# Three reorderings on VectorE in a bidirectional-WKV plus FFN kernel: four partial-weight sums, a backward scan and a low-half operand change places with their neighbours

## The reference

```python
ek  = exp(min(f, 30));  ekv = ek * f                 # k = v = f
n_t = n_{t-1} * decay + ekv_t                        # scans over time, forwards and backwards;
d_t = d_{t-1} * decay + ek_t                         # decay is one number per batch row and channel
num = nf + nb - ekv + exp(min(u + f, 30)) * f
den = df + db - ek  + exp(min(u + f, 30))
mix = sigmoid(x) * num / max(den, 1e-8) * (0.8 + 0.2 * tf)
h   = einsum('bsd,fd->bsf', mix, W1)
a   = gelu(clip(round(h / 0.1), -32768, 32767) * 0.1)
out = x + einsum('bsf,df->bsd', a, W2)
```

## Time and profile before

| | us |
|---|---|
| median of 2 runs | 1725.78 (1725.59 to 1725.98) |
| the profiled execution, its own time | 1725.98 |
| its span, first to last instruction | 1724.2 |
| PE busy in the span | 1628.7 |
| DVE busy | 1344.5 |
| ACT busy | 1027.1 |
| mean granted TensorE clock | 0.988 |

### The profile page before, as it was taken

How to read it: one execution, slowest core, us unless ns; L and a number is a source line. 1 busy time by engine, 2 the same in 40 slices (tenths; PEclk the granted TensorE clock), 3 DMA queues, 4 the chain that set the end, 5 groups by cost and what they waited for, 6 DMA issues and landing times. The chain is left out here.

```text
span 1724.2 us, 34213 instructions
## 1 busy us (share of the span) xinstructions
PE 1628.7 (94%) x13682; PEld 1341.6 (78%) x13682; DVE 1344.5 (78%) x1839; ACT 1027.1 (60%) x1635; POOL 162.2 (9%) x159
## 2 busy tenths in 40 slices
PE   1699999989899999999899999999989999999998
PEld 0234446878788888888788888888878888888887
DVE  8988796679878788698986789788987778946252
ACT  3578332655857666576756647576584757656361
POOL 0000110001020110101010020200102010110201
PEclk9799999999999999999999999999999999999999
DMA  8979985779576785959668695877958678586866
GB/s 238 250 177 297 305 307 194 252 252 286 167 183 233 226 259 152 262 179 285 207 178 242 199 263 178 196 255 216 276 164 227 205 226 243 159 263 225 217 193 132
DMA packets 163654, 386.63 MB, mean 224 GB/s; under 512 B 15200, under 2 KB 73312, under 8 KB 162528
## 3 DMA queue, kind: packets, MB, share of 16 engines
q1 hardware_dynamic: 116720, 291.29, 50.4%
q0 software_dynamic: 33200, 53.23, 18.3%
q10 hardware_dynamic: 13568, 39.85, 6.9%
HBM read 353.90 MB, written 85.98 MB: 255 GB/s over the span
## 5 line engine op out<-in xcount | busy, mean ns | idle before, releaser
L843 PE MATMUL ps<-mo,w_ring 128*128 128x256 f16 x6272 | 696.1, 273 | 10.3 <-DVE ps L1879 5.5
L843 PEld LDWEIGHTS ps<-mo,w_ring 128*128 128x128 f16 x6272 | 612.4, 98 | 85.7 <-issue 14.8
L906 PE MATMUL ps<-act,w_ring 128*128 128x256 f16 x5488 | 623.0, 275 | 22.8 <-DVE act L1958 17.7
L906 PEld LDWEIGHTS ps<-act,w_ring 128*128 128x128 f16 x5488 | 539.9, 99 | 94.2 <-DVE act L1958 19.8
L758 POOL DMA_DIRECT2D out_dram<-xy x111 | 134.6, 1360 | 1339.0 <-ACT xy L1324 773.5
L1879 DVE SCALAR_TENSOR_TENSOR ps<-sp,ps 128x512 f32<-128x512 f32 x84 | 58.1, 692 | 113.6 <-PE ps L843 61.6
L1266 ACT ACTIVATE a<-q 128x1024 f32<-128x1024 int16 x124 | 130.9, 1056 | 6.7 <-DVE act L1919 2.1
L1958 DVE SCALAR_TENSOR_TENSOR act<-tt,act 128x1024 f16<-128x1024 f32 x91 | 110.9, 1218 | 12.4 <-ACT act L1307 12.4
L784 PE MATMUL ps<-mo,w_ring 128*128 128x512 f16 x256 | 66.1, 422 | 55.6 <-DVE mo L1808 55.2
L1013 PE MATMUL ps<-act,w_ring 128*128 128x512 f16 x512 | 110.7, 379 | 0.0
L1932 DVE TENSOR_TENSOR tt<-a 128x1024 f32<-128x1024 f32 x49 | 59.9, 1223 | 61.6 <-ACT a L1266 61.6
(11 more groups left out here) (139 smaller groups left out, 1902.2 us busy)
## 6 DMA issues: line engine op xcount, KB each, us to landing
w_ring<-w1s SPq DMA_DIRECT2D x168, 512.0 KB, 5.7
w_ring<-w_half SPq DMA_DIRECT2D x74, 512.0 KB, 6.0
w_ring<-w2s SPq DMA_DIRECT2D x56, 512.0 KB, 5.1
out_dram<-xy POOLq DMA_DIRECT2D x111, 256.0 KB, 6.3
w_ring<-w2f SPq DMA_DIRECT2D x56, 384.0 KB, 4.3
V<-in_fside_dram SPq DMA_DIRECT2D x64, 256.0 KB, 4.9
R<-in_x_dram SPq DMA_DIRECT2D x64, 256.0 KB, 5.2
w_half<-in_w_dram POOLq DMA_DIRECT2D x16, 1024.0 KB, 9.9
```

The source lines that it names most:

```text
L843: mm = pe.matmul(dst[:, f, :], wp_ring[:, k, r, f, q, :], mo[:, op, q, p, :], start=(fresh and f == 0 and q == 0 and p == 0), stop=(q == K ...
L906: mm = pe.matmul(dst[:, i, :], wy_ring[:, k, i, 2 * (s - base) + j, :], ab[:, operand_at(s, op), j, p, :], start=(fresh and i == 0 and s = ...
```

## The change

In VectorE's `chained_block` three pairs of neighbours change places. Nothing is added or removed, and the lists of the other engines stay as they are.

- Edit 1, block 1 only: in the rounds s = 2, 3 and 4 `f_sums(s - 2)` comes ahead of `seed_u4(hid(n, s))`, no longer behind it. (`f_sums(3)` stays.)
- Edit 2, all blocks (it has an effect in 1 to 6): `mix(5, 2)` comes ahead of `seed_u4(hid(n, 6))`.
- Edit 3, all blocks (it has an effect in 1 to 6): `quads_lo_11(n, 6)` comes ahead of `mix(6, 1)`.

```diff
                     mix(1, s - 2)
+                    if n == 1:
+                        f_sums(s - 2)
                     if not nxt:
                         check(at + 2 * s - 4)
                         check(at + 2 * s - 3)
                     seed_u4(hid(n, s))
-                    if n == 1:
-                        f_sums(s - 2)
...
                 check(at + 3 if nxt else at + 8)
+                mix(5, 2)
                 seed_u4(hid(n, SPLIT + 2))
-                mix(5, 2)
                 mix(5, 3)
...
                 mix(6, 0)
                 seed_u4(hid(n, LAST))
+                quads_lo_11(n, SPLIT + 2)
                 mix(6, 1)
-                quads_lo_11(n, SPLIT + 2)
                 quad_sums(n, SPLIT + 2)
```

## The result

| | before | after |
|---|---|---|
| median of the runs, us | 1725.78 (2 runs) | 1739.66 (2 runs, 1738.90 to 1740.41) |
| the profiled execution, its own time | 1725.98 | 1740.08 |
| its span | 1724.2 | 1738.2 |
| mean granted TensorE clock | 0.988 | 0.981 |

The ratio is 1.0085, with an interval of 1.0060 to 1.0109: 13.9 us more, where 17.2 us were forecast. The time of 1739.7 us lies inside the range, 3.3 us under the predicted number. Of its terms, edit 3's was right in kind and size, edit 1's 3.6 us did not come at all, and the clock's 1.6 us and edit 2's gain of 0.6 us were both far too small. That the total came so near is in part luck, as the steps show further on.

What follows compares the result with a forecast made beforehand. TensorE, 94% busy, loses only by its waits, largest for T1, where ScalarE sets the pace. Edits 2 and 3 (12.0 us), edit 1 (3.6) and clock (1.6) add 17.2 us to 1725.8: 1743.0 us, range 1735 to 1754.

Steps and rivals of the forecast that it cites:

- edit 1's 3.6 us: Block 1: late seeds behind sums that wait for stores cost 3.6 us, between 2.0 and 5.0.
- the clock's 1.6 us: Block 6: T1's wait grows to about 4.1 us, adding one clock fall of 1.6 us.
- 2.20 and 2.01 us per block: Edit 3: T1 comes 2.20 us later in blocks 1, 3, 5 and 2.01 us later in 2, 4, 6.
- Rival D: Edit 3: `quad_sums` waits for the gelu anyway, so it costs 7 us at most; 1738 us in sum; 5%.
- rival A: ScalarE's copy is ready when `seed_u4(n, 7)` ends, so VectorE's idle time is won: 1720 us; 4%.
- The waits of 2.0 us: Edit 2: TensorE waits about 2.0 us ahead of `products_73(n, 6)` in blocks 1, 3, 5, covered by T1's wait.
- 0.1 us per block: Edit 2: the wait of about 0.14 us behind `backward`'s copy is hidden, taking 0.1 us per block off edit 3.
- the seed starts at 342.37: Block 1, s = 3: the seed behind `f_sums(1)`, whose stores land at 340.3, starts at 342.37 plus some 0.4 us.
- rival C: Edit 1 costs nothing, its waits covered by 2.30 us before `y_15_end(1, 0)` and load waits: 1739 us; 14%.
- the wait of 4.6 us: Block 1, edit 1: TensorE waits 4.6 us ahead of `products_73(3)`, and the clock falls there.
- block 1 growing by less than 4 us: Sign that the prediction is wrong: block 1 grows by less than 4 us or by more than 8.
- rival B: The clock falls for longer: seven lengthened waits at 1.6 us add 11 us, 1754 us; 12%.

Runs made afterwards that it cites:

- edit 3 alone: Only edit 3, `quads_lo_11(n, 6)` ahead of `mix(6, 1)`, made to the kernel before: 1746.77 us, ratio 1.0115.
- `forward` behind: Kernel before with `quads_lo_11(n, 6)` first, as in edit 3, but `mix(6, 1)` moved behind `quantise22(n, 7)`: 1731.01 us, ratio 1.0027.
- edit 2 alone: Only edit 2, `mix(5, 2)` ahead of `seed_u4(hid(n, 6))`, made to the kernel before: 1719.95 us, ratio 0.9963.
- edits 1 and 2: The change without edit 3, against the kernel before: 1721.05 us, ratio 0.9972.
- s = 3 and 4 alone: Edit 1 only in the rounds s = 3 and 4, made to the kernel before: 1729.29 us, ratio 1.0022.
- s = 2: Edit 1 only in the round s = 2, made to the kernel before: 1723.99 us, ratio 0.9985.
- 2 and 3: The change without edit 1, against the kernel before: 1739.94 us, ratio 1.0080.

## Why the prediction was right, and where not, by its steps

**Edit 3, right in mechanism and size.** 2.20 and 2.01 us per block were worked out, 2.12 and 1.93 us were measured with edit 3 alone. The chain holds link by link: idle time of 3.51 us ended by the same copy, no idle time ahead of `quad_sums`, T1's wait lengthened by as much. The kernel with `forward` behind the chain confirms that it is `forward` in this place which costs. Rival D (the 0.88 us still to be taken off) is refuted by this size, and rival A (copy ready earlier) by the 3.51 us: `quads_lo_11`, which the copy releases, starts 4.20 us after `seed_u4(3, 7)` in block 3 both before and after.

**Edit 2, right in the wait, wrong in the sum.** The waits of 2.0 us were there (1.67 us in blocks 3 and 5, 1.87 us in block 1), T1's wait covered them, and with the cover gone the edit does cost. But the edit isn't near nothing: the term "0.1 us per block" measured 0.25 us in odd and 0.26 to 0.54 us in even blocks. In the odd ones the hidden wait behind the copy was right and sized too small. In the even ones the step left out VectorE's own wait of 0.47 us for product 6 ahead of the seed, which moving the seed back hides. The prediction also gave edit 2 no part of the clock. The profile of edit 2 alone has 4.8 us there, 3.2 of them in the even blocks, where T1's wait fell to 1.65 us; the pair of edits 1 and 2 doesn't show it again.

**Edit 1, wrong.** 3.6 us predicted, 0 measured (13.8 us without it, 13.9 us with it; alone: 0 within 2 us). The step that failed is the one that kept the landing time of `f_store(0)` at 8.6 us: "the seed starts at 342.37". With `products_73(2)` delayed by 2.0 us, the load and the copy that had run beside those stores came behind them, and `f_sums(1)` started 4.5 us after their issue, at 338.01 us and not at 340.8. That took 1.82, 0.55 and 2.30 us of TensorE's waits away, which paid for the 2.0 us of s = 2. Where this didn't happen (s = 3 and 4 alone) the chain cost 3.6 us. So rival C (edit 1 costs nothing) is what came, but by another way than it said: the wait of 4.6 us was not covered, it didn't arise. The prediction named block 1 growing by less than 4 us as a sign that it is wrong. Block 1 grew by 0.5 us, so by its own sign it failed there. The 2.1 us for edits 2 and 3 in block 1 are missing from its length too: T1's wait did grow by 2.11 us, and `y_15_end(1, 2)` came 1.95 us sooner, of which edit 2 alone had 0.6 us in its profile. What brought the rest is open.

**The clock, mis-sized.** One fall more was added, 1.6 us. Measured are 5.4 us, and 7.3 us with edit 3 alone. Block 6 does fall now, as said (2.74 us in place of 0). What the step missed is that places that fell before can lose more when the wait ahead of them is longer: the 1.3 to 1.6 us of blocks 1 to 5 became 1.4 to 2.6 us. That is rival B in kind, at about half of its price. The fall of the clock at the 4.6 us wait, which is inside edit 1's 3.6 us, had no wait to follow. In the kernels of this study, grouped by T1's wait:

| T1's wait, us | kernels and blocks | slow matmuls behind it | rows of 56 longer by, us, where slow | mean of all, us |
|---|---|---|---|---|
| 1.64 to 1.93 | edit 2, edits 1 and 2; even | 1 of 6 | 1.7 | 0.3 |
| 2.17 to 2.19 | before, 1, s = 2, s = 3 and 4, `forward` behind; even | 9 of 15 | 1.5 to 1.6 | 0.9 |
| 3.56 to 4.11 | after, 3, 2 and 3; even | 9 of 9 | 1.2 to 2.8 | 2.2 |
| 3.65 | before, 1, 2, 1 and 2, s = 2, s = 3 and 4, `forward` behind; odd | 20 of 21 | mostly 1.2 to 1.7, up to 2.8 | 1.6 |
| 5.76 | after, 3, 2 and 3; odd | 9 of 9 | 1.8 to 2.6 | 2.2 |

In blocks of one kind the mean loss grows with the wait: 0.3, 0.9 and 2.2 us in the even ones, 1.6 and 2.2 us in the odd ones. But 3.6 to 4.1 us in an even block cost as much as 5.76 us in an odd one. The length of the wait alone doesn't price a fall; what else does is not shown. (The prediction's 1739.8 us without the clock takes edit 1 at 2.0 us; its own working, 2.3 us, gives 1740.1.)

**Why the total was near all the same.** Of the predicted 17.2 us, 15.6 us were waits (12.0 and 3.6) and 1.6 us clock. The profile after holds 8.8 us of waits (8.3 and 0.5 in block 7) and 5.4 us of clock. The waits were 6.8 us too many: 5.5 of the 5.7 us predicted for block 1 (2.1 for edits 2 and 3 there, 3.6 for edit 1) are missing, and 1.8 us in blocks 2 to 6, where edit 2's gain was put too low. The 0.5 us of block 7, which was to stay as before, go the other way. The clock was 3.8 us too little. What is left, 3.0 us, is the miss of the total: two errors of different sign, 6.8 and 3.8 us, of which the smaller hid as much of the larger. That is luck and no merit of the sum.

The Trainium skill (TensorE: Matmul & The Clock Gate, section "HAM oscillation — how this bites in real kernels") tells of a kernel whose wait between two bursts of matmuls sent the array back to half rate every single time. The trace agrees at waits of 3.6 us and more (38 of 39 followed by slow matmuls); at 2.17 us it was 9 of 15 and at 1.6 to 1.9 us 1 of 6.

## What to carry to other kernels

An instruction that is moved from ahead of an in-order engine's wait to behind it costs its length, less the idle time that the engine still has further on in the same chain. Here these were 3.18 us of `forward` less 0.98 us, 2.20 us worked out and 2.12 us measured. A wait put in elsewhere is free while a later wait covers it, and that one covers only if what it waits for doesn't come later too: edit 2 brought 6 us with T1's wait behind it, and cost 3.4 us where only the 4.11 us wait for `y22` was left. Where TensorE waits in every block, give the clock a term of its own, for each place and with the length of its wait: 12 us of added waits took 7.3 us of clock with them. A landing time read from a trace holds for the traffic that was in flight there, so see which transfers move along before it is used for a moved store.

## What the runs showed of the hardware that was not expected

- Two stores of one sort: the instruction that waits for them started 8.6 to 8.7 us after the first was issued in the seven kernels where a weight load and a copy in DRAM were issued within 0.4 us of it, and 4.4 to 5.3 us after in the seven where these were issued 1.64 us behind or later.
- In block 3 after a wait of 5.76 us the granted clock was 0.50 over 3 us and 0.61 over the next, where it had been 0.91 after 3.65 us. The 56 matmuls took 8.2 to 8.95 us after 5.76 us, in place of 6.37, and mostly 7.6 to 8.0 us after 3.65 us. But the longest rows, 9.1 to 9.2 us, came after waits of 3.56 to 4.11 us, so the longest wait did not give the longest slow stretch. In the even blocks of the kernel before, with the same wait of 2.17 us, they took 7.95 us twice and 6.37 us once.
